# A two-layer MoE and attention kernel on one core: the scores of two head pairs ahead of V, another order behind attention, and part of the expert sums on VectorE

## What is computed

```python
x = x + moe0(group_norm(x))        # 8 experts, inner 512, gelu, top 2 of softmax; plus a shared gated expert
t = tokens(x)                      # 4 images of 256 tokens
t = t + attention(layer_norm(t))   # 12 heads of 16; below
t = t + moe1(layer_norm(t))        # 16 experts, inner 384, silu(x wg) * (x wu) wd, top 2; plus a shared one

# attention, per image and head
att = softmax(q @ k.T * 16 ** -0.5)
att = softmax(att * mask)          # mask: 0.5 where token numbers agree modulo 64, else 1
out = (att @ v) @ w_out + b_out
# top 2 of both expert layers: weights of the two best, divided by their sum
```

## Time and profile before

| what | us |
|---|---|
| median of 3 runs (481.32, 486.88, 487.42) | 486.88 |
| the profiled execution: time | 480.29 |
| the profiled execution: span | 478.5 |
| PE busy | 431.8 (90%) |
| DVE busy | 223.3 (47%) |
| ACT busy | 156.7 (33%) |
| POOL busy | 125.1 (26%) |

### The profile page before, as it was taken

How to read it: one execution, slowest core, us unless ns; L and a number is a source line. 1 busy time by engine, 2 the same in 40 slices (tenths; PEclk the granted TensorE clock), 3 DMA queues, 4 the chain that set the end, 5 groups by cost and what they waited for, 6 DMA issues and landing times.

```text
span 478.5 us, 7595 instructions
## 1 busy us (share of the span) xinstructions
PE 431.8 (90%) x2321; PEld 308.4 (64%) x2322; DVE 223.3 (47%) x597; ACT 156.7 (33%) x394; POOL 125.1 (26%) x136
## 2 busy tenths in 40 slices
PE   0999889999999997888888779798999999999995
PEld 0755366666678886665666556446677777777775
DVE  4455342222221775789899753551443333333322
ACT  2024322222221152798787733003222221222110
POOL 3201135554551000000000000002255554444430
PEclk9999999999999999699999999869999999999999
DMA  8989011111002891000000661910011001110006
GB/s 234 264 317 276 10 34 42 43 36 40 30 17 85 227 363 76 0 1 1 3 1 0 156 142 44 269 51 8 22 35 32 22 24 36 33 31 22 0 1 197
DMA packets 18056, 38.62 MB, mean 81 GB/s; under 512 B 4420, under 2 KB 13892, under 8 KB 17586
## 3 DMA queue, kind: packets, MB, share of 16 engines
q1 hardware_dynamic: 10610, 30.45, 22.5%
q0 software_dynamic: 5280, 6.32, 4.7%
q10 hardware_dynamic: 2144, 1.57, 1.1%
HBM read 35.16 MB, written 7.67 MB: 90 GB/s over the span
## 4 chain that ended last, share of the span: by engine, by line
PE 82%; ACT 7%; DVE 4%; DMA 4%; issue 2%; DVEq 0%; SPq 0%; POOLq 0%; ACTq 0%
PE bank L1182 17%; PE bank L1197 13%; PE bank L1118 12%; PE bank L1176 8%; PE bank L1360 5%; PE bank L1189 4%; PE bank L1320 3%; PE bank L1374 3%; PE bank L1158 2%; PE bank L1104 2%; PE bank L1151 2%; ACT xn_t L673 2%; ACT scratch L673 2%; ACT g_sh L673 2%; DMA w_first<-y_rows 2%
## 5 line engine op out<-in xcount | busy, mean ns | idle before, releaser
L1182 PE MATMUL bank<-w_first,rows_t 96*128 x248 | 85.4, 487 | 0.8 <-ACT rows_t L596 0.6
L503 POOL DMA_INDIRECT rows<-xn_rows,slot_tok x56 | 57.3, 1022 | 99.8 <-DVE slot_tok L830 42.5
L511 POOL DMA_INDIRECT y_rows<-y,slot_row x54 | 55.2, 1023 | 99.0 <-DVE y L882 58.5
L1197 PE MATMUL bank<-w_second,hid_t 128*128 x370 | 70.1, 329 | 4.7 <-DVE hid_t L867 2.8
L1197 PEld LDWEIGHTS bank<-w_second,hid_t 128*128 128x128 f32 x370 | 58.7, 190 | 7.2 <-issue 7.1
L1182 PEld LDWEIGHTS bank<-w_first,rows_t 96*128 96x128 f32 x248 | 44.6, 190 | 26.1 <-issue 1.3
L872 DVE TENSOR_TENSOR act_h<-bank,act_g 128x384 f32<-128x384 f32 x31 | 17.3, 558 | 63.7 <-PE bank L1182 63.7
L1176 PE MATMUL bank<-w_first,rows_t 96*128 (+1 forms) x92 | 43.5, 594 | 1.1 <-issue 1.0
L664 ACT ACTIVATE scratch<-bank,neg_max 128x256 f32<-128x256 f32 x96 | 44.0, 478 | 0.9 <-DVE neg_max L987 0.8
L1005 DVE SCALAR_TENSOR_TENSOR scratch<-scratch,exp_inv,const 128x256 f32<-128x256 f32 x96 | 40.2, 481 | 0.8
L549 POOL COPY act_h<-o_inv 128x256 f32<-128x256 f32 x12 | 4.8, 401 | 131.1 <-DVE o_inv L1015 131.1
(11 more groups left out here) (175 smaller groups left out, 620.0 us busy)
## 6 DMA issues: line engine op xcount, KB each, us to landing
w_first<-in_gate_up SPq DMA_DIRECT2D x16, 576.0 KB, 10.0
w_second<-in_down SPq DMA_DIRECT2D x1, 4608.0 KB, 23.9
w_first<-in_fc SPq DMA_DIRECT2D x1, 3072.0 KB
w_second<-in_fc SPq DMA_DIRECT2D x1, 3072.0 KB, 28.2
xn_rows<-xn_tok SPq DMA_DIRECT2D x2, 768.0 KB, 9.5
rows<-xn_rows,slot_tok POOLq DMA_INDIRECT x56, 2.6
y_rows<-y,slot_row POOLq DMA_INDIRECT x54, 2.3
w_first<-in_x_t SPq DMA_DIRECT2D x2, 384.0 KB, 4.5
```

The lines of the kernel that those rows point to most:

```text
L503: pool.indirect_dma_start(rows[b % 2][:], None, xn_rows[L.l], bass.IndirectOffsetOnAxis(slot_tok[:, b:b + 1].bitcast(U32), 0), bounds_chec ...
L511: pool.indirect_dma_start(y_rows[L.l], bass.IndirectOffsetOnAxis(slot_row[:, b:b + 1].bitcast(U32), 0), y[b % 2][:], None, bounds_check=TO ...
L1182: ins = pe.matmul(bank[:, 5 + g, 0:I1], rows_t[0:CH, k, :], w(CH, (k * 2 + g) * I1, I1), start=(k == 0), stop=(k == NCH - 1))
L1197: ins = pe.matmul(bank[:, 1, 0:C], hid_t[:, tile(ic)], w(P, ic * C, C), start=(ic == 0), stop=(ic == L.IC - 1))
```

## The change

1. Two pairs' scores stand ahead of V: PE runs `scores(0)` and `scores(1)` as soon as ten of the twelve parts of Q and K are ready, then three of V's products, `scores(2)`, and the fourth. V's four copies go from DVE to ACT, between the first exponentials, and ACT first runs an exponential of one column that nobody reads (`exp_first`). Two of the three buffers `e1` move from `scratch` to the front of `w_first`; the weights of experts 0 and 1 (`LATE` is 2) are therefore loaded at attention's end and not with the first batch.
2. From attention's last chunk to L1's blocks: the shared expert's first pieces no longer stand ahead of the last projection and of the second half's transposes; the first half's transposes go behind the projection. ACT takes the square root ahead of the last chunk's copy, DVE normalizes ahead of `out_norm`. The best two are found in halves (`best0`, `best1`), so the logits of tile 4 wait for the first half's copy. In L1 `count` stands behind three pieces instead of five, `slots` behind seven of the twelve instead of eleven, `at_place` is made in quarters, and `out2` goes behind the blocks. The store of `xn_rows` goes from SP to ACT's queue, and the last six weight loads wait for the last projection instead of the normalized rows.
3. DVE adds the experts' rows itself (`add_own`, two instructions a tile) for tiles 2 and 3 of L0 and 1, 3 and 5 of L1; the other tiles stay on PE.

```diff
+        e1 = [w_first[:, o:o + 4 * TOKENS_IMG].rearrange("p (a b) -> p a b", a=4)
+              for o in (0, 4 * TOKENS_IMG)] + [scratch_at(2048, 4, TOKENS_IMG)]
+        LATE = -(-2 * 4 * TOKENS_IMG // per_expert)
...
             0: (["logits", ...
-                ["top2", 0, "pads", 1, ...
+                ["best0", "best1", "top2", 0, "pads", 1, ...
-            1: ([(2, 0), "count", (2, 1), "rank", (3, 0), "expert", (3, 1), (4, 0), (4, 1), (5, 0), "slots",
-                 (5, 1), "out0", "out1", "out2", "first rows"],
-                [0, "top2", 1, "pads", 2, "ended", "expert", "blocks", "places", 3, "slots", 4, 5, "weights"]),
+            1: ([(0, 1), (1, 0), "count", (1, 1), "rank", (2, 0), (2, 1), "expert", (3, 0), "slots", (3, 1), (4, 0),
+                 (4, 1), (5, 0), (5, 1), "first rows", "out0", "out1"],
+                ["best0", "best1", "top2", "pads", 0, "ended", "blocks", "places", "expert", 1, "slots", 2, 3,
+                 "weights", 4, 5]),
+        OWN = ((2, 3), (1, 3, 5))
+        SUM_ORDER = ((2, 3, 0, 1, 4, 5, 6, 7), (1, 3, 5, 0, 2, 4, 6, 7))
...
-            for e in range(EARLY):
+            for e in range(LATE, EARLY):
                 sp.dma_start(wg_up[:, e], d["gate_up"][:, e]).then_inc(s_w1a, 16)
...
-            sp.wait_ge(xn_tok_ready, 2 * NT)
-            sp.dma_start(by_tile(xn_rows[1]), xn_tok[:]).then_inc(xn_stored, 16)
+            sp.wait_ge(att_t_ps, N_PAIRS - 1)
+            for e in range(LATE):
+                sp.dma_start(wg_up[:, e], d["gate_up"][:, e]).then_inc(s_w1a, 16)
+            sp.wait_ge(proj_ps, IMAGES)
             for e in range(MIDDLE, E1):
...
-            act.wait_ge(v_ps, NT // 2)
+            def value_copy(n):
+                act.wait_ge(v_ps, n + 1)
+                nc.scalar.copy(v_tok[:, 2 * n:2 * n + 2, :, 0:D].rearrange("p j h d -> p (j h) d"),
+                               bank[:, 6 + n % 2, 0:2 * C].rearrange("p (m d) -> p m d", d=D)).then_inc(v_out, 1)
+            act.wait_ge(filled, 1)
+            nc.scalar.activation(exp_first[:], ones[:, 0:1], ACT.Exp)
+            value_copy(0)
             exp_scores(0)
+            value_copy(1)
             exp_scores(1)
+            value_copy(2)
+            value_copy(3)
             for p in STEPS:
                 if p + 2 < N_PAIRS:
                     exp_scores(p + 2)
+                if p == N_PAIRS:
+                    act_std(act, 2, 0)
...
-            act_std(act, 2, 0)
             act_norm_transposes(act, 2, (0, 1))
             act_std(act, 2, 1)
-            act_shared(act, L1, 0)
             act_norm_transposes(act, 2, (2, 3))
-            for s in range(1, 2 * L1.IC):
+            act.wait_ge(xn_tok_ready, 2 * NT)
+            act.dma_start(by_tile(xn_rows[1]), xn_tok[:]).then_inc(xn_stored, 16)
+            for s in range(2 * L1.IC):
                 act_shared(act, L1, s)
-            act.wait_ge(L1.gap_ready, 1)
-            nc.scalar.activation(gap_e[:], gap[:], ACT.Exp).then_inc(L1.gap_exp, 1)
+                if s == 1:
+                    act.wait_ge(L1.gap_ready, 1)
+                    nc.scalar.activation(gap_e[:], gap[:], ACT.Exp).then_inc(L1.gap_exp, 1)
...
+            def add_own(L, js):
+                tiles = NT // len(y_back[L.l])
+                dve.wait_ge(L.y_in[js[0] // tiles], 16 * TOPK)
+                first = TOPK * OWN[L.l].index(js[0])
+                for k in range(TOPK):
+                    for i, j in enumerate(js):
+                        if k == 0:
+                            dve.wait_ge(L.sum_ready, sum_no(L, j))
+                        else:
+                            dve.wait_ge(L.own_sums, first + i + 1)
+                        v.scalar_tensor_tensor(x_tok[:, j, :], y_back[L.l][j // tiles][:, k, j % tiles, :],
+                                               weight[:, k, j:j + 1], x_tok[:, j, :], ALU.mult, ALU.add
+                                               ).then_inc(L.own_sums, 1)
...
-            for j in range(NT // 2):
+            for j in OWN[0]:
+                add_tile(L0, j)
+            add_own(L0, OWN[0])
+            for j in (0, 1):
                 add_tile(L0, j)
...
-            neg_maximum(2)
             for p in STEPS:
                 if p < N_PAIRS:
                     attention(p)
+                if p == 0:
+                    neg_maximum(2)
                 if p == N_PAIRS:
                     ln_stats(0)
-                if p == N_PAIRS + 2:
-                    ln_rows(2, 0)
                 if chunk_at(p, SUMS) is not None:
                     invert_sums(chunk_at(p, SUMS))
+                if p == N_PAIRS + 1:
+                    ln_rows(2, 0)
...
+                if j == NT // 2:
+                    pe.wait_ge(L.logits_read, 1)
...
-            pe.wait_ge(parts_ready, 2 * QKC)
+            pe.wait_ge(parts_ready, QKC + 4)
             scores(0)
             scores(1)
-            pe.wait_ge(v_out, NT // 2)
+            for n in range(3):
+                values(n)
+            pe.wait_ge(parts_ready, 2 * QKC)
+            scores(2)
+            values(3)
...
             chunk_stages(N_PAIRS)
-            keep_busy(2)
+            keep_busy(1)
             chunk_stages(N_PAIRS + 1)
             keep_busy(2)
-            norm_transposes(2, 0)
             chunk_stages(N_PAIRS + 2)
             keep_busy(1)
+            chunk_stages(N_PAIRS + 3)
+            norm_transposes(2, 0)
+            keep_busy(2)
             pe.wait_ge(tp_out, NT + 2)
             pe.wait_ge(s_sh1, 32)
-            shared(L1, 0, 0)
-            chunk_stages(N_PAIRS + 3)
-            shared(L1, 0, 1)
             pe.wait_ge(s_gate1, 32)
             for j in range(NT // 2):
                 logits(L1, j)
-            shared(L1, 1, 0)
             pe.wait_ge(x_new, IMAGES)
             norm_transposes(2, 1)
-            shared(L1, 1, 1)
+            shared(L1, 0, 0)
```

More of the change, by code:

```diff
@@ L322, in build @@
         q_high = [act_h, hid_t]
-        e1 = [scratch_at(1024 * i, 4, TOKENS_IMG) for i in range(3)]
+        e1 = [w_first[:, o:o + 4 * TOKENS_IMG].rearrange("p (a b) -> p a b", a=4)
+              for o in (0, 4 * TOKENS_IMG)] + [scratch_at(2048, 4, TOKENS_IMG)]
+        LATE = -(-2 * 4 * TOKENS_IMG // per_expert)
         p2_t = [scratch_at(3072, 4, TOKENS_IMG),
@@ L740, in route @@
                 E, NBP = L.E, L.NB + 1
-                if stage == "top2":
-                    dve.wait_ge(L.logits_ps, 2)
-                    lg = logit[:, :, 0:E]
-                    go(v.tensor_copy(lg, bank[:, 3, 0:NT * E].rearrange("p (j e) -> p j e", e=E)))
-                    for j in range(NT):
+                if stage in ("best0", "best1"):
+                    half = int(stage[-1])
+                    tiles = range(half * NT // 2, (half + 1) * NT // 2)
+                    dve.wait_ge(L.logits_ps, half + 1)
+                    v.tensor_copy(logit[:, tiles[0]:tiles[-1] + 1, 0:E],
+                                  bank[:, 3, tiles[0] * E:(tiles[-1] + 1) * E].rearrange("p (j e) -> p j e", e=E)
+                                  ).then_inc(L.logits_read, 1)
+                    dve.wait_ge(L.logits_read, half + 1)
+                    for j in tiles:
                         step(v.max(top8[:, j, :], logit[:, j, 0:E]))
                     join()
-                    for j in range(NT):
+                    for j in tiles:
                         step(v.max_index(top8i[:, j, :], top8[:, j, :], logit[:, j, 0:E]))
+                elif stage == "top2":
                     v.tensor_tensor(gap[:], top8[:, :, 1], top8[:, :, 0], ALU.subtract).then_inc(L.gap_ready, 1)
@@ L821, in route @@
                     n = TOPK * NT
-                    v.tensor_tensor(at_place[:], bc(iota, 1, [P, n, P]), bc(slot_f[:, 0, :], 2, [P, n, P]),
-                                    ALU.is_equal).then_inc(L.at_place_ready, 1)
+                    for m in range(0, n, n // 4):
+                        m = slice(m, m + n // 4)
+                        v.tensor_tensor(at_place[:, m], bc(iota, 1, [P, n // 4, P]),
+                                        bc(slot_f[:, 0, m], 2, [P, n // 4, P]), ALU.is_equal
+                                        ).then_inc(L.at_place_ready, 1)
                 elif stage == "slots":
@@ L1053, in _ @@
             blocks(L1)
-            for j in range(NT):
+            for j in OWN[1]:
+                add_tile(L1, j)
+            for j in OWN[1]:
+                add_own(L1, (j,))
+                add_tile(L1, j - 1)
+            for j in (6, 7):
                 add_tile(L1, j)
@@ L1139, in out_tile @@
                     pe.wait_ge(L.y_ready, L.NB)
+                own = j in OWN[L.l]
                 for ic in range(L.IC):
-                    pe.matmul(sum_at(L, j), L.hid[half][ic][:, tile(j % (NT // 2))], w[:, ic, :],
-                              start=(ic == 0), stop=False)
+                    ins = pe.matmul(sum_at(L, j), L.hid[half][ic][:, tile(j % (NT // 2))], w[:, ic, :],
```

(17 more changed lines are left out.)

26 lines of the change are left out of this document (14 added, 12 removed).

## The result

| | before | after |
|---|---|---|
| median, us | 481.44 (476.38 to 487.42, 5 runs) | 462.72 (462.35 to 467.23, 5 runs) |
| profiled execution: time, span | 480.29, 478.5 | 467.23, 465.4 |
| mean granted clock | 0.975 in the profiled execution | 1.00 in four, 0.989 in the profiled one |

The profiled execution of the kernel before is a sixth one, beside the five. The ratio is 0.9646, with a 95% interval of 0.9599 to 0.9693: 3.5% faster. The prediction was 461.0, range 455 to 471.

A forecast was written before the change was run, and what follows sets the result against it. PE, busy 90% of the span, was taken as the bound where it stands still or runs slow. 478.5 - 7.1 - 10.3 - 1.1 - 0.9 + 0.4 = 459.5, with 1.8 outside the span 461.3; likeliest 461, range 455 to 471.

The forecast's parts named there:

- Part 1: Attention's start, scores ahead of V: `exp_att(0)` comes 7.1 us earlier, bounds 5.2 and 8.0.
- no cost of the table switch beyond 1.28: ACT at attention's start: the table load takes 1.28 us, and no drain of about 1.38 is added.
- Part 2: From attention's end to the last layer's blocks: 10.3 us gained, 3.0 of it at the projection; bounds 3.5 and 11.5.
- The clock behind the count: Last layer, ahead of the blocks: 13.6 us at half speed lose 6.8 us, gained if PE keeps its clock.
- the count's wait: PE's wait for DVE's part of the routing in the last layer: 2.64 us go.
- the last product's wait: PE between attention and blocks: a wait of 1.0 us goes, covered by the first rows' transposes.
- the new wait ahead of the second half's transposes: Behind the last projection: an added wait for the first half's copies and normalized rows, about 0.6 us.
- `out2` behind the blocks: 1.0 us leaves the way to the blocks and costs nothing where PE waits 2.03 for the last loads.
- Part 3: DVE's own sums: 1.1 us gained at the end, bounds 0 and 1.9, and 0.9 in the first layer.
- The split logits: First layer: logits of tile 4 wait for a copy of the first four, 0.4 us lost, 0 to 0.8.
- The low clock stays: Rival: the clock still falls at attention's start and behind the count, giving 470 us; chance 0.17.
- The runs' other 6 us stay: Rival: what separates 487 from 481 lies where the change doesn't touch, so the median is 467; chance 0.13.

The follow-up runs named there:

- p1_only: The kernel before with only the first item of the change; 476.35 us, ratio 0.9889.
- A: First profiled execution of the changed kernel, the slowest of its five: 467.23 us, span 465.4, clock 0.989.
- p1_filled: The kernel before with the first item of the change and four idle matmuls in PE's wait for the count; 469.19 us, ratio 0.9734.
- B: Second profiled execution of the changed kernel, unaltered: span 461.1 us, clock 1.00.
- steady: The changed kernel with one more idle matmul at each of two places ahead of 286 us; 462.63 us, ratio 0.9643.
- p3_only: The kernel before with only the third item of the change; 477.77 us, ratio 0.9895.
- before_filled: The kernel before with eight idle matmuls in PE's wait for the first exponentials and four in its wait for the count; 476.47 us, ratio 0.9895.

## Why the prediction was right

**Part 1** held step by step: `exp_att(0)` at 192.21 for 192.4, and 7.1 us in p1_only. Two assumptions carried it, a copy on ACT at 0.48 and no cost of the table switch beyond 1.28, and both were measured. Most of these 7 us is order, not clock. Half of the 9.6 us at 1.2 GHz would be 4.8, but PE stood idle for nearly the first 3 us of that stretch, as it waited until 193.05. The first row, a stretch of the kernel before, shows the clock falling while PE is at 0.00; the other two are the scores and the transposes in its chain, beside the `keep_busy` of 2.00:

```profile
190.00:191.00 1.00, 0.00 (x0) 0.00 (x0) 0.73 (x1) 0.99 (x2) 0.00 (x0) 0.62 0.00 0
```

```profile
194.78 1.22 PE bank L1334 x8
...
198.01 1.72 PE bank L1360 x8
```

A has 0.67, 1.06 and 0.89 for these three, so the clock accounts for at most 2.3 us of the gain, and the other 5 or so come from the new order.

**Part 2** held as well: the projection 3.0 earlier as predicted, and 34.23 us from there to the first block for 33.9. The clock behind the count was worth 6.5 (6.8 predicted). All the rest of the stretch's terms, the count's wait, the last product's wait and `out2` against what was added, came to a net 0.5 in the prediction and to 0.6 by p1_filled against B. Not each of them held: the wait for the last product was to be covered, and 0.77 of its 1.0 is still there, while the new wait ahead of the second half's transposes was 0.25 for the 0.6 taken. `out2` behind the blocks cost nothing there (133.02 for 133.14). The moved queues did no harm: the store of `xn_rows` took 12.9 us to land from ACT's queue, but from 286.38, so it was there by 299.3, and the first gather came at 310.

**Part 3** was mis-sized at the end. The step "so tiles 6 and 7 can't be added before 473.5 and end at 475.0. Gain 1.1" let the last load land 6.9 after the last scatter and 1.5 of work follow it. In A it landed 7.5 after, behind three queued issues, and 2.07 followed: PE's two tiles in 1.55, then DVE's last addition. In B the load on the chain landed 6.2 after, and three tiles followed it in 2.95. The gain was -0.1 in A and 0.3 in B. In the first layer 0.9 was predicted. From L0's last result to `exp_att(0)` the three kernels with part 1 and without part 3 took 44.5 to 45.1, the changed kernel and steady 43.7 to 44.1: 0.4 to 1.4. The split logits showed their wait, 0.38 where 0.4 was predicted. The +1.52 in the table is mostly something else: over the profiles of five kernels without the split that point lies at 147.62 to 149.21, and the profile of before was the earliest.

**The rivals.** "The low clock stays" was not what happened in its two places, but a fall of 10.4 us appeared in a third, in one of eleven executions. What the prediction set against it, the wait of 2.03 at 470 us that left the clock at 1.00, was in part luck of that execution: behind the same wait, of 2.11, 2.00 and 2.09, the clock fell in the profiles of p1_only, p1_filled and p3_only. "The runs' other 6 us stay" failed in its condition: by p3_only's profile two thirds of them were longer low stretches in the two places that the change touches, and the rest stood at the last sums. In eight of eleven executions of the changed kernel neither is left. The page that was cited with it (by the Trainium skill, TensorE: Matmul & The Clock Gate, Part 1: The HAM clock gate, the number of slow matmuls varies from run to run) was the better guide: the 46 executions from 0.965 to 0.986 agree with it.

**The sum.** The prediction counted 19.0 us from the profiled execution, and B shows 17.4; 1.1 of the difference is L0's start and 0.8 the last sums, less 0.3 from attention's loop. The median of before is 481.44, not 486.88, so the gain is 18.7. How much of it is clock can be worked out in three ways. By the chain it is at most 2.3 and 6.5, some 9 of B's 17.4. The straight line has the kernel before at 470.6 at full clock, which makes it 11. before_filled at full clock took 473.0 and 474.2, which makes it 7 to 8, with what the fill itself costs. So 7 to 11 of the 18.7 us are the clock that came back, and the rest is waits and order. That the median fell so near to the forecast also owes something to chance: the sum counted 1.6 us too much in the profiled execution, while the median of before lies 1.2 above that execution.

## What to carry over

Where PE's granted clock falls behind a wait, price that wait with half of PE's work on the chain in the low stretch that follows, not with half of the stretch: behind the count 13.6 us at 1.2 GHz cost 6.5, at attention's start 9.6 us cost at most 2.3. Before reordering, try a few idle matmuls in the wait: four of them gave back those 6.5, while eight in the other wait did not hold the clock. The scatter of a kernel's own times can be the same low stretch in different lengths: plot time against mean clock before looking for another cause. And when a summing engine is relieved at the end, count from the landing of the last load and the work that must follow it, since that load becomes the bound at once.

## What was unexpected of the hardware

The clock fell at 286 us in A though PE had been 79 to 100% busy in each of the three microseconds before and had waited 0.51 at most. In before_filled it fell behind waits of 0.92 and 1.09, and in the kernel before the wait of 2.03 at 470 us left it at 1.00. Behind the same wait it fell in p1_only (2.11), p1_filled (2.00) and p3_only (2.09), and in steady behind 1.40. The length of the last wait alone doesn't tell whether it falls. Loads of `y_rows` of the same size took between 3.49 (before, the first one waited for) and 5.97 us (A, the last).
